# Graph attention on one core: the first five chosen tiles made inside the projection, and the first source scores spread by a transfer

## The reference

```python
h = relu(layernorm(x)); x = x + smooth(h, adj)         # step 1, two big products with adj
h = relu(layernorm(x))                                 # step 2
Wh = einsum('nf,hfd->hnd', h, W)                       # the projection
e_src = einsum('hnd,hd->hn', Wh, a1)
e_dst = einsum('hnd,hd->hn', Wh, a2)
e = leaky_relu(e_src[:, :, None] + e_dst[:, None, :], 0.2)
att = softmax(where(adj > 0, e, -9e15))                # per head, over all 2048 columns
enc = elu(einsum('hnm,hmd->hnd', att, Wh))             # attention
x = x + mlp(enc)                                       # four dense layers
```

## Time and profile before

| what | us |
|---|---|
| median of 3 runs | 868.38 |
| lowest and highest run | 867.96, 868.98 |
| span of the profiled execution, first to last instruction | 866.6 |
| TensorE busy in that span | 845.1 |
| VectorE busy | 703.7 |
| ScalarE busy | 424.1 |
| GpSimd busy | 280.2 |

### The profile page before, as it was taken

The page is one execution under the profiler, slowest core; times in us unless marked ns, Lnnn a source line. Parts: engine busy times, 40 slices in busy tenths (PEclk is TensorE's granted clock), DMA queues, the critical chain, the costliest instruction groups (busy, mean ns, idle before and its releaser), DMA issues.

```text
span 866.6 us, 15265 instructions
## 1 busy us (share of the span) xinstructions
PE 845.1 (98%) x5211; PEld 759.2 (88%) x5211; DVE 703.7 (81%) x1223; ACT 424.1 (49%) x782; POOL 280.2 (32%) x298
## 2 busy tenths in 40 slices
PE   2999999999999999999999999999999999999998
PEld 2888888888888888888799999999999999999776
DVE  6899886557656885596999999999999999999864
ACT  3445333321111112255676666666666666775753
POOL 0000000000000000067676555555566644566332
PEclk9999999999999999999999999999999999999999
DMA  8979822703222222050250000000010032000144
GB/s 346 406 273 370 351 97 71 196 0 121 97 97 98 97 97 73 2 194 3 65 187 18 21 25 26 26 24 24 26 26 25 24 87 72 26 2 8 43 147 148
DMA packets 37338, 87.44 MB, mean 101 GB/s; under 512 B 7136, under 2 KB 8288, under 8 KB 37280
## 3 DMA queue, kind: packets, MB, share of 16 engines
q1 hardware_dynamic: 37280, 86.72, 28.7%
HBM read 73.93 MB, written 12.78 MB: 100 GB/s over the span
## 4 chain that ended last, share of the span: by engine, by line
PE 95%; DVE 2%; ACT 1%; DMA 1%; issue 0%; DVEq 0%
PE bank L1754 29%; PE bank L77 15%; PE bank L79 15%; PE bank L78 15%; PE bank L1788 14%; PE bank L554 3%; PE bank L2321 1%; PE bank L977 1%; PE bank L2315 1%; PE bank L2317 1%; PE bank L2260 1%; DMA l_h<-x 1%; DVE l_stats L228 0%; DVE wh L2124 0%; ACT l_last_neg L2206 0%
## 5 line engine op out<-in xcount | busy, mean ns | idle before, releaser
L1316 DVE SCALAR_TENSOR_TENSOR l_q<-bank,neg_d,mask 128x512 fp32r<-128x512 f32 x512 | 338.6, 741 | 23.0 <-PE bank L1754 23.0
L1754 PE MATMUL bank<-l_parts,l_q 128*128 128x260 f32 x2048 | 252.1, 284 | 0.8 <-DVE l_q L1316 0.7
L1754 PEld LDWEIGHTS bank<-l_parts,l_q 128*128 128x128 f32 x2048 | 248.5, 189 | 2.3 <-POOL l_parts L1653 0.9
L77 PE MATMUL bank<-x_hi,s_hi 128*128 128x512 f32 x448 | 174.5, 389 | 0.0
L79 PE MATMUL bank<-x_hi,s_lo 128*128 128x512 f32 x448 | 174.3, 389 | 0.0
L78 PE MATMUL bank<-x_lo,s_hi 128*128 128x512 f32 x448 | 174.3, 389 | 0.0
L776 POOL TENSOR_TENSOR l_prod<-wh,l_a 128x512 f32<-128x512 f32 x29 | 34.6, 1212 | 382.4 <-ACT wh L741 382.4
L1491 ACT ACTIVATE l_mask<-mask 128x512 fp32r<-128x512 uint8 (+1 forms) x256 | 136.5, 620 | 0.1
L1788 PE MATMUL bank<-l_parts,l_mask 128*128 128x260 f32 x1024 | 127.3, 284 | 0.0
L1788 PEld LDWEIGHTS bank<-l_parts,l_mask 128*128 128x128 f32 x1024 | 125.7, 189 | 0.0
L79 PEld LDWEIGHTS bank<-x_hi,s_lo 128*128 128x128 f32 x448 | 84.1, 188 | 17.6
(11 more groups left out here) (224 smaller groups left out, 1129.4 us busy)
## 6 DMA issues: line engine op xcount, KB each, us to landing
rows<-adj_t SPq DMA_DIRECT2D x48, 512.0 KB, 3.8
l_now<-adj SPq DMA_DIRECT2D x16, 512.0 KB, 7.3
l_rows_k<-adj_t SPq DMA_DIRECT2D x16, 512.0 KB, 8.1
l_src<-e_rows SPq DMA_DIRECT2D x30, 256.0 KB, 3.1
l_kept<-adj SPq DMA_DIRECT2D x12, 512.0 KB, 13.2
wh_store<-wh SPq DMA_DIRECT2D x1, 4160.0 KB, 15.6
l_h<-x SPq DMA_DIRECT2D x4, 1024.0 KB, 17.3
x<-x SPq DMA_DIRECT2D x1, 4096.0 KB, 13.6
```

What stands on the lines that cost most here:

```text
L77: pe.matmul(acc, hi, rhs_hi, start=first, stop=False, skip_group_check=True)
L1316: v.scalar_tensor_tensor(out=q[:, i, :], in0=bank[S_BANKS[hh]][:], scalar=neg_d[:, i, h:h + 1], in1=mask[:, i, cols], op0=ALU.is_ge, op1=A ...
L1754: return pe.matmul(bank[Q_BANKS[hh][t]][:, 0:PW], q[:, i, t * P:(t + 1) * P], parts[pair_slot][:, i, hh * PW:(hh + 1) * PW], start=i == 0, ...
```

## The change

- `choose` for round 0, head 0 is cut in two. Its tiles 0 to 4 are made in steps 11 to 15 of the projection, one in each, between `cut_turned` and `reduce_e` on VectorE. Tiles 5 to 15 stay where all 16 were.
- For that the negated destination scores `neg_d` are made in two halves, the near half in step 10, the far half where the whole was.
- `sel`, its two copies and the two spreading matmuls go. In their place SyncE loads the two rows of `e_rows` for round 0 right after the first quarter's store, and ScalarE fills bank 6 at the head of its step 10 (`EARLY_Q - 1`), and bank 7 after `last_wh`.
- `turn_e` of tiles 0 to 3 moves from step 8 to step 7, `take_e_t(0)` from step 9 to step 8.
- The buffers of attention move, so that `q` and `src` lie clear of what the projection still uses; GpSimd gets two waits for the stores out of `e_t`.

```diff
@@ sync
-                sp.dma_start(e_rows[:, cols], e_t[:, cols]).then_inc(stored, 16)
-            sp.wait_ge(stored, 64)
+                sp.dma_start(e_rows[:, cols], e_t[:, cols]).then_inc(stored if q else first_stored, 16)
+                if q == 0:
+                    sp.wait_ge(first_stored, 16)
+                    first_scores()              # load_src(0): two broadcast loads
+            sp.wait_ge(stored, 48)
@@ scalar, loop over in_turns(T, (normalise, 0), (cut_turned, 1), (take_early_wh, 2))
+                if k == EARLY_Q - 1:
+                    a.wait_ge(x1_done, T)
+                    first_scores()              # fill_src(0, 0)
@@ vector
+            def early_q(t, b):
+                if t == EARLY_Q - 1:
+                    v.wait_ge(e_ready, 2 * G8 + 4)
+                    v.tensor_scalar(neg_d[:, NEAR, :], d_m[:, NEAR, :], -1.0, None, ALU.mult).then_inc(chain, 1)
+                elif t >= EARLY_Q:
+                    if t == EARLY_Q:
+                        v.wait_ge(chain, 1)
+                    choose_early(t - EARLY_Q)
-            for k in in_turns(T, (cut_turned, 0), (late_chain, 0), (reduce_e, 2)):
+            for k in in_turns(T, (cut_turned, 0), (late_chain, 0), (early_q, 0), (reduce_e, 2)):
...
-                if k == G8:
-                    for hh in range(2):
-                        v.tensor_copy(sel[:, hh, :], ident[0:2 * H, hh:hh + 1].to_broadcast([2 * H, P])
-                                      ).then_inc(sel_ready, 1)
-                if k in (9, 13):
-                    take_e_t((k - 9) // 4)
+                if k in (8, 13):
+                    take_e_t((k - 8) // 4)
@@ tensor
-                if k in (8, 12, 16):
+                if k in (7, 12, 16):
...
-            pe.wait_ge(sel_ready, 2)
-            pe.wait_ge(e_copied, 1)
-            for hh in range(2):
-                pe.matmul(bank[6 + hh][:], sel[:, hh, :], e_t[:, 0:512], start=True, stop=True
-                          ).then_inc(src_spread, 1)
@@ attention, vector
-                choose(0, 0, 0, slice(0, QW), {G8: lambda: v.wait_ge(src_spread, 2), ...})
+                choose(0, 0, 0, slice(0, QW), tiles=range(T - early_q, T))      # tiles 5 to 15
@@ attention, scalar
                 last_wh(a)
+                a.wait_ge(e_ready, 2 * T + 4)
+                fill_src(0, 1)
@@ attention, gpsimd
+                p.wait_ge(first_stored, 16)
                 for half in halves:
                     p.tensor_tensor(first_whole[2][:, half, :], ...)
...
+                p.wait_ge(stored, 48)
                 p.tensor_tensor(first_whole[3], ...)
@@ attention, tensor
-                pe.wait_ge(first_lo, 2)
+                pe.wait_ge(first_lo, 1)
+                pe.wait_ge(first_a_lo, 1)
```

More of the change, by code:

```diff
@@ L630, in spread_and_project @@
         norm_ready = sem("l1_norm_ready")
-        e_t = rows[0:2 * H, 0:2, :].rearrange("p b n -> p (b n)")
-        h2 = rows[:, 2, :].rearrange("p (b f) -> p b f", b=2)
+        e_t = rows[0:2 * H, 2:4, :].rearrange("p b n -> p (b n)")
+        h2 = rows[:, 1, :].rearrange("p (b f) -> p b f", b=2)
         dst_top = sb("l2_dst_top", [P, 1, H], side="right")
@@ L955, in vector @@
             v.tensor_copy(top_w[:], top[:].to_broadcast([H, P])).then_inc(top_ready, 1)
-            v.tensor_scalar(neg_d[:], d_m, -1.0, None, ALU.mult).then_inc(chain, 1)
+            v.tensor_scalar(neg_d[:, FAR, :], d_m[:, FAR, :], -1.0, None, ALU.mult).then_inc(chain, 1)
             v.wait_ge(top_steps, 3)
@@ L966, in args_summed @@
         def args_summed(v):
-            v.wait_ge(chain, 2)
+            v.wait_ge(chain, 3)
         def late_args(v):
@@ L1132, in attend_and_finish @@
         parts = (parts_even, parts_odd)
+        o_q = [sb(f"l4_o_q{hh}", [P, GT, PW]) for hh in range(2)]
+        sb("l4_to_src", [P, 96])
+        src = sb("l4_src", [P, 2, QW])
+        o_m = sb("l4_o_m", [P, GT, PW])
         (whole,), (last_neg, _) = one_place(
@@ L1135, in attend_and_finish @@
             [("l5_last_neg", [P, 2, H, HD], F32), ("l5_rest_whole", [P, T], F32)])
-        o_q = [sb(f"l4_o_q{hh}", [P, GT, PW]) for hh in range(2)]
-        o_m = sb("l4_o_m", [P, GT, PW])
+        share = sb("l5_share", [P, T * H, 1])
+        fine = sb("l5_fine", [P, T * H, 1])
+        sb("l4_to_q", [P, 736])
+        (q,), (hi_odd, lo_odd, o1_hi, o1_lo) = one_place(
+            nc, ctx, [("l4_q", [P, T, QW], F32R)],
+            [("l5_enc_t_hi1", [P, KC, QW], F32R), ("l5_enc_t_lo1", [P, KC, QW], F32R),
+             ("l5_o1_hi", [P, 2, K1, QW], F32R), ("l5_o1_lo", [P, 2, K1, QW], F32R)])
         def as_whole(tile):
@@ L1240, in combine @@
             return first_head, second_head
-        (programs, (third_scores, args_summed, late_args, last_wh, late_factors, late_scores), (src_spread, wh_summed, wh_ready, chain),
-         x1_stored, stored, fac_ready) = before
+        (programs, (third_scores, args_summed, late_args, last_wh, late_factors, late_scores), (wh_summed, wh_ready, chain, e_ready),
+         x1_stored, (first_stored, stored), fac_ready, early_q) = before
         WH_READY = T + 2
@@ L1298, in _, with choose @@
             def _(v):
-                vector_before(v)
-                v.wait_ge(x1_stored, 16)
-                def choose(r, hp, hh, cols, between={}):
+                def choose(r, hp, hh, cols, between={}, tiles=range(T)):
                     h, u = 2 * hp + hh, 2 * r + hh
-                    for i in range(T):
+                    at_start = isinstance(u, int) and u == 0
+                    for i in tiles:
                         if i in between:
                             between[i]()
-                        if i < T - QUAD:
+                        if at_start:
+                            pass
+                        elif i < T - QUAD:
                             v.wait_ge(q_done, T * u + i + 1)
@@ L1311, in choose @@
                             v.wait_ge(q_done, T * u + T)
[L1312 to L1314 removed]
+                        if i == 0:
                             v.wait_ge(src_filled, u + 3)
@@ L1318, in choose @@
                                                op0=ALU.is_ge, op1=ALU.mult).then_inc(q_ready, 1)
+                vector_before(v, lambda i: choose(0, 0, 0, slice(0, QW), tiles=(i,)))
+                v.wait_ge(x1_stored, 16)
                 quarter = slice(0, QUAD)
@@ L1509, in cut_quarter @@
                                  ACT.Copy).then_inc(first_hi, 1)
+                a.sem_inc(src_filled, 2)
+                scalar_before(a, lambda: fill_src(0, 0))
+                a.wait_ge(x1_stored, 16)
+                a.sem_inc(q_bank_free, GT)
+                a.sem_inc(m_bank_free, GT)
                 a.wait_ge(wh_summed, WH_READY)
-                a.wait_ge(chain, 3)
+                a.wait_ge(chain, 4)
                 cut_quarter(0, 0)
```

68 lines of the change are left out of this document (28 added, 40 removed).

## The result

The changed kernel took 871.92 us (median of 4 runs, 871.15 to 873.82) against 868.17 us for the kernel before on the same chip: a ratio of 1.0048 (95% interval 1.0036 to 1.0060), 3.75 us slower. The forecast was 870.3, so 1.95 us slower. In a second set of runs the changed kernel stood at 1.0044 (1.0030 to 1.0057). The profiled execution is the slowest of the first four: 873.82, with a span of 871.9. The likeness of 871.92 and 871.9 is chance: the one is the median time, the other the span of the slowest execution.

The account below looks back on a forecast made before the run. TensorE, busy 98% of the span, was taken to bound the kernel. A 2.05 us stall in step 10 less 0.1 at attention's start gave +1.95 us, from 868.38 to 870.3 us, range 868.2 to 872.1.

Parts of the forecast that it names:

- Part 1: Projection, steps 11 to 15: five early tiles at 0.66 us each and half of `neg_d` hide in VectorE's idle time; cost nothing.
- Part 2: Attention's start: the spreading matmuls' 1.98 us become idle time, so TensorE starts only 0.1 us earlier, at most 0.3.
- Part 3: First `q_phase`: of 2.75 us only about 0.1 comes through, since `m_phase` then waits for GpSimd's rest; bounds 0 and 0.7.
- Part 4: Projection step 10: ScalarE waits for the load before filling bank 6, runs 2.8 us late, and TensorE loses 2.05 us.
- I take 3.7: Step 10's transfer: the first of the two loads assumed to land 3.7 us after issue, as in the trace's pair.
- the sum: Whole kernel: +2.05 for step 10's stall, -0.1 for attention's start, +1.95 us in all.
- The stated bounds of 3.0 and 3.7: Step 10's transfer: landing time in us from issue, 3.0 as for a lone load, 3.7 as for the first of a pair.
- The rival of the lone load: Step 10's transfer: the first load lands after 3.0 us as if alone, loss 1.35 us, time 869.6; chance 0.15.
- Part 5: Attention's moved buffers: worth 0.3 us either way over 16 rounds, taken as 0; GpSimd's two new waits cost nothing.
- the clock: Projection, behind step 10's stall: 3.41 us at half pace would cost 1.7 us more, time 872.0; a rival, chance 0.13.
- a stretch 1.96 us busy near the end that did not bring it down: Trace of the kernel before: cited in the forecast as a stretch with 1.96 us busy where the granted clock stayed up.
- the same fall at attention's start costs nothing: Attention's start: a fall to half clock is free, covered by about a microsecond of waiting for `second_lo`.

Follow-up runs that it names:

- the kernel with the later fill: The changed kernel with ScalarE filling bank 6 at the head of its step 11 instead of step 10; 868.86 us, ratio 1.0010 to the kernel before.
- the kernel with the stall filled: The changed kernel plus seven idle-time TensorE matmuls into unread bank 7 in step 10; 871.25 us, ratio 1.0038 to the kernel before.

## Why the prediction was wrong in size, step by step

- **Part 1, tiles hidden in the projection: right.** The ruler of the kernel with the later fill is that of the kernel before.
- **Part 2, attention starts 0.1 earlier: right in kind.** L1032 to the first product is 4.12 us in the kernel with the later fill against 4.38, so 0.26, within the 0.3 allowed.
- **Part 3, nothing comes through: right in its main point, one term missed.** `m_phase` waits for GpSimd's rest of the second head; taking the early tiles away changed nothing, taking work off GpSimd gained 1.1 us. What I left out is that GpSimd's lateness also reaches VectorE at its cast (4.27 us idle with the later fill), and that this slows the next `q_phase` (15.83 us for its 126 matmuls against 15.52): L1032 to round 1's `m_phase` is 38.82 us with the later fill against 38.58, 0.24 more although the first `m_phase` starts no later.
- **Part 4, the stall: right, up to 0.4 too small.** Place, order and times held within 0.3 us up to the load. "I take 3.7" was 4.0 in the first trace and 3.6 in the second, so the loss was 2.44 and 2.07 (an estimate) where the sum has 2.05. The stated bounds of 3.0 and 3.7 were too narrow above. That the pair slows itself, which the forecast rested on, was shown by holding the second back. The rival of the lone load is out.
- **Part 5, buffers: right.**
- **The step that failed is that the clock stood among the rivals, at 0.13, and not in the sum.** It fell behind the stall in both profiled executions of the changed kernel and cost 1.46 us there by the ruler in the first of them, and about 1.56 in the second; by the medians it was 0.7 to 0.9. The evidence that I set against it, a stretch 1.96 us busy near the end that did not bring it down, did not bear it: the stretches with the stall were busy for 1.44 and 1.81 us of 3.40, and the clock fell. And "the same fall at attention's start costs nothing" holds for one low stretch of some 3.4 us: L1032 to the first `m_phase` is 14.51 us with it (the kernel with the stall filled) and without it (the changed kernel run again). For 6.82 us the first `q_phase` took 11.3 us, which ran over the cover.
- **A second term was mis-sized as well: attention's start.** The sum has -0.1 for it; with the stall taken away the kernel was 0.84 us slower than before. The traces place 0.24 of that.

The sum as it stands now: 2.1 to 2.4 (the wait) + 0.7 to 0.9 by the medians for the clock + 0.84 (attention's start and what follows) is 3.6 to 4.2, against 3.75 and 3.92 measured in the two sets. The last two terms are differences of medians themselves, so this shows that the terms fit together and is no independent check. Of the 0.84, VectorE's late return explains 0.24. Part of the rest may be the slow clock at attention's start (0.24 by the medians when it was held up), but that lies within the scatter; the remainder is open. The spans behind the last `m_phase` vary from 84.5 to 85.5 us between profiled executions, too much to place a few tenths there.

## What to carry to other kernels

Making the inputs of the next stage early pays only if they are what that stage waits for next; read off who is second in line before moving anything, here GpSimd's chain, and then who is third. A wait placed in an in-order queue is priced by the slack of everything behind it: one instruction a step later was worth 3.2 us, and the early start could have been had without the stall. And where a stall leaves TensorE idle for 1.6 to 2.0 us in a dense stretch, as here, the price of the slow clock behind it belongs into the sum, not among the mishaps.

## What the runs showed of the hardware that was not expected

- The granted clock fell behind a stretch in which TensorE was busy 1.44 of 3.40 us (1.81 of 3.40 in the second execution profiled). It stayed up where seven matmuls whose result nobody used brought the busy time to 3.21 of 3.50 us; they were worth 0.7 to 0.9 us by the medians and 1.46 by the ruler. That agrees with what the Trainium skill says (TensorE: Matmul & The Clock Gate, The HAM clock gate), that activity is what releases the throttle.
- A low clock at attention's start came and went with the same program: in the changed kernel it lasted 6.8 us in one profiled execution and did not come in the other. In the kernel before it lasted 3.41 us.
- Two broadcast loads of 256 KB issued 0.4 us apart, each from one row of HBM, landed after 3.6 to 4.1 us (the first, in ten profiled executions), and after 3.2 us when each was alone.
